# Bias products of the first half moved behind its conditioning passes, with the selection tree in SBUF and a reordered last step

## The reference, cut to what matters

```
w = weights[subjects]; b = bias[subjects]
h = einsum('bct,bcd->bdt', x, w) + b[:, :, None]
gate = silu((h @ q(gate_w)) * gate_scale)
up = (h @ q(up_w)) * up_scale
out = x + ((gate * up) @ q(down_w)) * down_scale     # q: round to float8_e4m3
```

## Time and profile before

| | us |
|---|---|
| time, median of 3 runs (lowest to highest) | 50.13 (50.04 to 50.27) |
| the profiled execution's own time | 50.52 |
| its span, first to last instruction | 48.6 |
| PE busy | 43.6 (90%) |
| DVE busy | 39.0 (80%) |
| ACT busy | 26.3 (54%) |
| POOL busy | 9.8 (20%) |

### The profile page before, as it was taken

How to read it: one execution, slowest core, us unless ns; L and a number is a source line. 1 busy time by engine, 2 the same in 40 slices (tenths; PEclk the granted TensorE clock), 3 DMA queues, 4 the chain that set the end, 5 groups by cost and what they waited for, 6 DMA issues and landing times.

```text
span 48.6 us, 678 instructions
## 1 busy us (share of the span) xinstructions
PE 43.6 (90%) x201; PEld 33.6 (69%) x201; DVE 39.0 (80%) x74; ACT 26.3 (54%) x45; POOL 9.8 (20%) x19
## 2 busy tenths in 40 slices
PE   1999899999999999999999999999999999998000
PEld 1331499997788878888788887888878888976000
DVE  2828899699899999899998999997659495985900
ACT  0945406984559684597319695631845728870000
POOL 3028904049910003930000000000000000370000
PEclk9999999999999999999999999999999999999997
DMA  0499999999950000000000000000000000028093
GB/s 0 101 316 391 357 390 379 416 410 414 410 223 7 0 0 0 0 0 0 0 0 13 7 0 0 0 0 0 0 0 0 0 0 7 0 89 332 10 333 99
DMA packets 2995, 5.71 MB, mean 118 GB/s; under 512 B 432, under 2 KB 1072, under 8 KB 2992
## 3 DMA queue, kind: packets, MB, share of 16 engines
q1 hardware_dynamic: 2704, 5.53, 30.9%
q10 hardware_dynamic: 288, 0.15, 1.1%
HBM read 4.63 MB, written 1.05 MB: 117 GB/s over the span
## 4 chain that ended last, share of the span: by engine, by line
PE 81%; DMA 5%; POOL 3%; DVE 2%; issue 1%; DVEq 1%; POOLq 0%
PE gu L552 46%; PE acc L560 23%; PE acc L525 8%; DMA const_in<-in_consts_dram 5%; PE acc L516 3%; DVE res L454 2%; POOL bias_tok L327 2%; DVEq L70 1%; POOL bias_r L320 1%; POOL bias_r L318 0%; POOLq L323 0%; POOLq L317 0%
## 5 line engine op out<-in xcount | busy, mean ns | idle before, releaser
L552 PE MATMUL gu<-h_hi,w_q 128*128 128x512 f32 (+1 forms) x52 | 15.2, 378 | 0.0
L552 PE MATMUL gu<-h_lo,w_q 128*128 128x512 f32 (+1 forms) x52 | 15.1, 377 | 0.0
L281 ACT CAST f_hi<-fuse 128x512 fp32r<-128x512 f32 (+1 forms) x13 | 7.6, 587 | 10.5 <-DVE fuse L441 10.5
L449 DVE TENSOR_TENSOR f_lo<-fuse,f_hi 128x512 fp32r<-128x512 f32 (+1 forms) x13 | 8.8, 675 | 3.2 <-ACT f_hi L281 3.2
L552 PEld LDWEIGHTS gu<-h_hi,w_q 128*128 128x128 f32 x52 | 9.5, 187 | 2.1
L552 PEld LDWEIGHTS gu<-h_lo,w_q 128*128 128x128 f32 x52 | 9.4, 187 | 2.2 <-DVE h_lo L421 0.2
L441 DVE SCALAR_TENSOR_TENSOR fuse<-gu,const_in,silu 128x512 f32<-128x512 f32 (+1 forms) x13 | 9.2, 706 | 0.4 <-ACT silu L274 0.4
L274 ACT ACTIVATE silu<-gu,const_in 128x512 f32<-128x512 f32 (+1 forms) x13 | 8.5, 651 | 1.1 <-PE gu L552 1.1
L560 PE MATMUL acc<-f_lo,w_q 128*128 128x512 f32 (+1 forms) x26 | 8.0, 381 | 0.0
L560 PE MATMUL acc<-f_hi,w_q 128*128 128x512 f32 (+1 forms) x26 | 7.8, 376 | 0.0
L239 ACT ACTIVATE w_big<-w_big,big_least 128x768 f32<-128x768 f32 (+2 forms) x8 | 6.2, 770 | 0.5 <-DVE w_big L358 0.5
(11 more groups left out here) (37 smaller groups left out, 24.7 us busy)
## 6 DMA issues: line engine op xcount, KB each, us to landing
w_in<-in_weights_dram SPq DMA_DIRECT2D x4, 384.0 KB, 6.2
x_tok<-in_x_by_time_dram SPq DMA_DIRECT2D x1, 1024.0 KB, 8.9
out_dram<-res SPq DMA_DIRECT2D x3, 256.0 KB, 2.1
x_sb<-in_x_dram SPq DMA_DIRECT2D x1, 512.0 KB, 3.6
w_in<-in_weights_dram SPq DMA_DIRECT2D x2, 256.0 KB, 4.0
x_sb<-in_x_dram SPq DMA_DIRECT2D x2, 256.0 KB, 4.2
w_in<-in_weights_dram SPq DMA_DIRECT2D x2, 128.0 KB, 4.9
const_in<-in_consts_dram SPq DMA_DIRECT2D x1, 151.0 KB, 2.4
```

Of the source, the lines that this page charges most:

```text
L281: nc.scalar.copy(f_hi[:, s % SLOTS, cols], fuse[:, s % SLOTS, cols]).then_inc(f_hi_made, 1)
L449: nc.vector.tensor_tensor(f_lo[:, s % SLOTS, cols], fuse[:, s % SLOTS, cols], f_hi[:, s % SLOTS, cols].bitcast(F32), ALU.subtract).then_in ...
L552: last = nc.tensor.matmul(gu[:, (s + q) % 2, part, cols], w_q[:, i, col:col + P], h[:, n, k, cols], start=(v == 0 and k == 0), stop=(v == ...
```

## The change

The first half's conditioning products now open the accumulator, its bias products stand behind them and close it, and `h_made` goes up after each of these bias products. Nine zero matmuls become eleven. Half 0's tree moves from PSUM to SBUF, its even part is shared between ACT (three of four pairs) and POOL (one), and one block of half 0's placement goes from ACT to POOL. The bias split moves from POOL to DVE, where one of the two mask operations goes away. POOL spreads the bias of half 0, places its block, and only then spreads that of half 1. In the last step both pieces of gate and up run without a break; `down` is reordered so that block b = 0 of the last half is complete before b = 1; `finish(0, 1)` stands behind DVE's last two subtractions, `y_sc` behind ACT's last two roundings, and the store of POOL's result is issued by ACT.

```diff
-    WARM = 9
+    WARM = 11
-        tree = [... for t in (gu_flat[:, 512:1024], tree_sb)]
+        tree = [tree_sb[:, n].rearrange("p (q g d) -> p q g d", g=GH, d=D) for n in range(HALVES)]
-        ACT_BLOCKS = ((0, 1), (0,))
-        POOL_BLOCKS = ((), (1, 2))
+        ACT_BLOCKS = ((0,), (0,))
+        POOL_BLOCKS = ((1,), (1, 2))
@@ sync
-            sp.wait_ge(res_pool, 1)
-            store(0, 0, TOK)
@@ scalar, front
-            for n in range(HALVES):
-                nc.scalar.copy(tree[n], cond_rep[:, :, 0]...).then_inc(tree_even[n], 1)
+            nc.scalar.copy(tree[0][:, 0:PAIRS - 1], cond_rep[:, 0:PAIRS - 1, 0]...).then_inc(tree_even[0], 1)
+            nc.scalar.copy(tree[1], cond_rep[:, :, 0]...).then_inc(tree_even[1], 1)
@@ scalar, last step
-            silu_of(s, 0, PIECES[0])
+            for q in range(LAST):
+                silu_of(s, q, PIECES[q])
+            for q in range(LAST):
+                round_of(s, q, PIECES[q])
             act.wait_ge(y0_made, 1)
             nc.scalar.activation(y_sc[:], acc[:, 0], ACT.Copy, scale=down_col[:, 0:1]).then_inc(y_scaled, 1)
-            silu_of(s, 1, PIECES[1])
-            for q in range(LAST):
-                round_of(s, q, PIECES[q])
+            act.wait_ge(res_pool, 1)
+            act.dma_start(out_rows[:, 0, 0:TOK], res[:, 0, 0]).then_inc(stored, 16)
@@ gpsimd
-            nc.gpsimd.tensor_copy(bias_r[:], bias_in).then_inc(bias_hi_made, 1)
-            nc.gpsimd.tensor_tensor(bias_r[LO_ROW:2 * LO_ROW], ..., ALU.subtract).then_inc(bias_lo_made, 1)
-            for n in range(HALVES):
-                place_bias(n)
+            nc.gpsimd.tensor_copy(tree[0][:, PAIRS - 1], cond_rep[:, PAIRS - 1, 0]...).then_inc(tree_even[0], 1)
+            place_bias(0)
+            place(0)
+            place_bias(1)
+            place(1)
@@ vector, front
+            nc.vector.tensor_copy(bias_r[:], bias_in).then_inc(bias_hi_made, 1)
+            nc.vector.tensor_tensor(bias_r[LO_ROW:2 * LO_ROW], ..., ALU.subtract).then_inc(bias_lo_made, 1)
-            for bits in (bits_ps, bits_sb):
-                nc.vector.tensor_tensor(bits[:], ..., ALU.bitwise_and).then_inc(bits_made, 1)
+            nc.vector.tensor_tensor(bits_ps, ..., ALU.bitwise_and).then_inc(bits_made, 1)
@@ vector, last step
-            fuse_of(s, 0, PIECES[0])
+            for q in range(LAST):
+                fuse_of(s, q, PIECES[q])
+            for q in range(LAST):
+                rest_of(s, q, PIECES[q])
             finish(0, 1)
-            fuse_of(s, 1, PIECES[1])
-            for q in range(LAST):
-                rest_of(s, q, PIECES[q])
@@ tensor, bias_of(n)
-                                     start=True, stop=False, skip_group_check=True)
+                    last = nc.tensor.matmul(..., start=(n == 1), stop=(n == 0), skip_group_check=True)
+                    if n == 0:
+                        last.then_inc(h_made, 1)
@@ tensor, condition(n)
-                                                start=False, stop=(g == GH - 1), skip_group_check=True)
-                    last.then_inc(h_made, 1)
+                                                start=(n == 0 and g == 0), stop=(n == 1 and g == GH - 1), ...)
+                    if n == 1:
+                        last.then_inc(h_made, 1)
-            for n in range(HALVES):
-                bias_of(n)
-                condition(n)
+            condition(0)
+            bias_of(0)
+            bias_of(1)
+            condition(1)
@@ tensor, last step
-            gate_up(s, 0, PIECES[0])
+            for q in range(LAST):
+                gate_up(s, q, PIECES[q])
             for b in range(TB):
                 down_block(s - 2, 0, b)
                 down_block(s - 2, 1, b).then_inc(y0_made, 1)
-            gate_up(s, 1, PIECES[1])
+            for v in range(2):
+                down_block(s - 1, v, 0)
             for q in range(LAST):
+                down_block(s, 0, 0, PIECES[q])
+                if q == LAST - 1:
+                    down_block(s - 1, 0, 1)
+                last = down_block(s, 1, 0, PIECES[q])
+            last.then_inc(y1_made, 1)
+            down_block(s - 1, 1, 1)
+            for v in range(2):
+                last = down_block(s, v, 1)
+            last.then_inc(y1_made, 1)
```

More of the change, by code:

```diff
@@ L97, in adaln_ffn @@
         cond_bd = sb("cond_bd", [P, G, P])
-        tree_sb = sb("tree_sb", [P, TOK])
-        bits_sb = sb("bits_sb", [P, BITS, G], I32)
+        tree_sb = sb("tree_sb", [P, HALVES, TOK])
         bias_r = sb("bias_r", [P, D], F32R)
@@ L116, in adaln_ffn @@
         warm_ps = gu[:, 0, 0]
-        gu_flat = gu.rearrange("p s w c -> p (s w c)")
-        tree = [t.rearrange("p (q g d) -> p q g d", g=GH, d=D) for t in (gu_flat[:, 512:1024], tree_sb)]
+        tree = [tree_sb[:, n].rearrange("p (q g d) -> p q g d", g=GH, d=D) for n in range(HALVES)]
         bits_ps = gu[:, 1, 1, 0:BITS * G].bitcast(I32).rearrange("p (k g) -> p k g", g=G)
@@ L244, in _ @@
             act.wait_ge(const_ld, 16)
-            for n in range(HALVES):
-                nc.scalar.copy(tree[n], cond_rep[:, :, 0].unsqueeze(2).to_broadcast([P, PAIRS, GH, D])
-                               ).then_inc(tree_even[n], 1)
+            nc.scalar.copy(tree[0][:, 0:PAIRS - 1], cond_rep[:, 0:PAIRS - 1, 0].unsqueeze(2).to_broadcast([P, PAIRS - 1, GH, D])
+                           ).then_inc(tree_even[0], 1)
+            nc.scalar.copy(tree[1], cond_rep[:, :, 0].unsqueeze(2).to_broadcast([P, PAIRS, GH, D])
+                           ).then_inc(tree_even[1], 1)
             def place(n):
@@ L317, in _ @@
             pool.wait_ge(const_ld, 16)
-            nc.gpsimd.tensor_copy(bias_r[:], bias_in).then_inc(bias_hi_made, 1)
[L319 to L323, removed]
+            nc.gpsimd.tensor_copy(tree[0][:, PAIRS - 1], cond_rep[:, PAIRS - 1, 0].unsqueeze(1).to_broadcast([P, GH, D])
+                                  ).then_inc(tree_even[0], 1)
             def place_bias(n):
@@ L329, in place_bias, with place @@
                                         ALU.mult).then_inc(bias_placed, 1)
-            for n in range(HALVES):
-                place_bias(n)
-            pool.wait_ge(bd_zeroed, 1)
[L336 to L340, removed]
+            def place(n):
+                pool.wait_ge(tree_level[n], BITS)
+                for j in POOL_BLOCKS[n]:
+                    nc.gpsimd.tensor_copy(*block_of(n, j)).then_inc(cond_placed[n], 1)
+                pool.wait_ge(cond_placed[n], J)
+            pool.wait_ge(bias_pick_made, 1)
+            pool.wait_ge(bias_lo_made, 1)
+            place_bias(0)
+            pool.wait_ge(bd_zeroed, 1)
+            pool.wait_ge(bias_placed, 1)
+            place(0)
+            place_bias(1)
+            pool.wait_ge(bias_placed, 2)
+            place(1)
             for e, (i, lo, hi) in enumerate(POOL_PIECES):
@@ L380, in _ @@
             nc.vector.tensor_copy(ones_r[:], ones_f[:]).then_inc(ones_made, 1)
-            dve.wait_ge(subj_in, 16)
-            dve.wait_ge(bit_set, BITS)
-            for bits in (bits_ps, bits_sb):
-                nc.vector.tensor_tensor(bits[:], subj_i[:, 0:G].unsqueeze(1).to_broadcast([P, BITS, G]),
-                                        bit_of[:].unsqueeze(2).to_broadcast([P, BITS, G]),
-                                        ALU.bitwise_and).then_inc(bits_made, 1)
+            dve.wait_ge(const_ld, 16)
+            nc.vector.tensor_copy(bias_r[:], bias_in).then_inc(bias_hi_made, 1)
+            dve.wait_ge(bias_hi_made, 1)
+            nc.vector.tensor_tensor(bias_r[LO_ROW:2 * LO_ROW], bias_in[LO_ROW:2 * LO_ROW],
+                                    bias_r[LO_ROW:2 * LO_ROW].bitcast(F32), ALU.subtract).then_inc(bias_lo_made, 1)
+            dve.wait_ge(subj_in, 16)
             dve.wait_ge(iota_made, 2)
@@ L391, in _ @@
                                     ALU.is_equal).then_inc(bias_pick_made, 1)
+            dve.wait_ge(bit_set, BITS)
+            nc.vector.tensor_tensor(bits_ps, subj_i[:, 0:G].unsqueeze(1).to_broadcast([P, BITS, G]),
+                                    bit_of[:].unsqueeze(2).to_broadcast([P, BITS, G]),
+                                    ALU.bitwise_and).then_inc(bits_made, 1)
             def select(n):
@@ L398, in select @@
                     if k == 0:
-                        dve.wait_ge(tree_even[n], 1)
+                        dve.wait_ge(tree_even[n], 2 - n)
                         to = tree[n]
@@ L406, in select @@
                         data = tree[n][:, step:PAIRS:2 * step]
-                    mask = (bits_sb if n == 0 and k > 0 else bits_ps)[:, k, groups].unsqueeze(1).unsqueeze(3).to_broadcast([P, left, GH, D])
+                    mask = bits_ps[:, k, groups].unsqueeze(1).unsqueeze(3).to_broadcast([P, left, GH, D])
                     nc.vector.copy_predicated(to, mask, data).then_inc(tree_level[n], 1)
-            dve.wait_ge(const_ld, 16)
-            dve.wait_ge(bits_made, 2)
+            dve.wait_ge(bits_made, 1)
             select(0)
```

(34 more changed lines are left out.)

## The result

| | before | after |
|---|---|---|
| time, median (lowest to highest) | 50.20 us (50.04 to 50.34) | 51.27 us (51.15 to 52.07) |
| ratio to before, 95% interval | | 1.0216 (1.0167 to 1.0265) |
| span of the profiled execution | 48.6 | 49.3 |
| its own time | 50.52 | 51.37 |

The change makes the kernel 1.07 us slower; 51.1 was forecast.

A forecast was written before the change was run, and what follows sets the result against it. The chain TensorE, ACT, DVE, TensorE ahead of the first gate product was taken to decide: front +1.05, tail -0.05, so 51.1 us on the median of 50.13. Range 50.5 to 51.45 us.

The forecast's parts named there:

- Start of conditioning: Half 0's conditioning on TensorE, set by half 0's placement: starts at about 6.1 us, 0.05 earlier (ends: 0.15 earlier, 0.3 later).
- The bias products: Moved behind half 0's conditioning, they delay ACT's copy of h and so the first gate product: +1.05 us (0.85 to 1.3).
- The sum: Profiled execution's own time 50.52 + 1.0 = 51.5; it lies 0.39 above the median of 50.13, so 51.1 on the median.
- The cover: TensorE's two further bias products (0.47 us) lie under ACT's delay; without that cover they would cost about 0.4.
- The tail: Last step: DVE's chain ends 0.67 us earlier, but final stores give back almost all: -0.05 (ends -0.67 and +0.1).
- The rate formula: End of span: when the last stores' data is ready, plus 1.8 us fixed, plus bytes over 377 GB/s; 48.55 forecast.
- A: Rival at the final stores: they don't bind, so the tail gives its 0.67 us; 50.5 us, chance 0.10.
- B: Rival: tail outweighs front, if `high_of_h(0, 0)` starts before 8.4 and the front costs under 0.67; 49.85 us, chance 0.04.
- C: Rival: TensorE's full clock comes later because it idles between the zeros and conditioning; 52.2 us, chance 0.05.
- D: Rival in half 0's placement: DVE and POOL lock each other out, or a late tree; +0.15, 51.25 us, chance 0.07.

## Why the prediction was right

**What decides.** The line that the forecast was built on, TensorE's eighth product, ACT's copy, `big(0)`, DVE's two passes, gate product, is the one that the trace of after shows. The move alone (+1.9%) and the changed kernel without it (+0.05%) frame it from both sides, and reordering ACT's list takes most of it off.

**Start of conditioning.** "About 6.1, 0.05 earlier": 6.05. The 0.05 can't be told from scatter: with the old front conditioning starts at 6.14, 6.11 and 6.04 in three traces, with the new one at 6.05 to 6.10. The masked copies start at 3.87 (3.85 forecast), the blocks are over by 5.99 (6.0). The Trainium skill's rule of a lock between DVE's and GpSimd's copies ("SBUF — State Buffer", Who interferes with whom) didn't show: POOL's copy ran from 5.58 to 5.89 beside DVE's two in 0.47 us. No run shows whether DVE's copies were in the two-port mode that the rule is about.

**The bias products.** +1.05 was forecast for the gate product. At equal pace the runs show +1.01 (11.27 against 10.26) or +0.96 (against 10.31, the old front with the stores spread). Against the trace of before it is only +0.63, and my absolute times of the front were 0.4 to 0.5 us late (ACT 8.84 forecast, 8.37 measured; idle ahead of `add_big(0)` 1.6 forecast, 1.12 measured), because of the one thing that I had left where it was: the moment at which TensorE reaches its upper clock. Of the zero matmuls still running at 4.7 us, the trace of after has

```profile
L515 PE MATMUL gu<-warm x3: 379/390/601, 4.4 to 5.0; 128*128 128x512 bf16 x3
```

(ns, shortest, median and longest), so the pace changes there at about 4.8 us, not 7. Conditioning ran wholly at 2.4 GHz, 1.8 us for sixteen products in place of the 2.21 of the earlier trace rows. It is no effect of the change, as the last section shows. The trace of before was the odd one: its span is 48.6 us, and 40 of the 46 executions of that kernel that were measured beside the experiments have 48.1 to 48.3. The sum had taken off 0.39 for that execution without knowing its cause. So the forecast of the median compares kernels on one footing, and the +1.05 holds there; the comparison of the two traces alone would not have shown it.

The cover named for TensorE's two further bias products was real. They "would cost by themselves about 0.4"; with ACT's order put right they cost about 0.3.

**The tail.** "DVE's chain ends 0.67 earlier": 0.70 between old and new tail in the changed kernel, and all four `finish` operations run on end, so DVE did wait for neither block, as forecast. Between the traces of before and after it is 0.63, and the 0.07 of difference is not the tail's: with the old tail in the changed kernel DVE ends 35.60 behind the first gate product, 35.53 in the kernel before. "The transfers give back almost all, -0.05": in the changed kernel the span behind the gate product is 38.01 with the old tail and 38.03 with the new one, so they give back all of it, as far as spans given to 0.1 us can tell. The rate formula held: `finish(0, 1)` ended at 43.86 + 0.75 = 44.61, and 44.61 + 1.8 + 2.78 (1.05 MB at 377 GB/s) is 49.2 against a span of 49.3; with one store less it gives 44.63 + 1.8 + 2.09 (0.79 MB) = 48.5 against 48.6. Its rate of 377 is the best half microsecond, though; from 45.5 to 48.0 it was 324 to 377. The Trainium skill's rule quoted beside it, that DMAs of both issuing engines share 16 engines and interleave ("Trainium Kernel Development and Optimization", Key Constraints), agrees with the trace: with stores of both queues under way the engines moved 373 GB/s at most, and 377 in the half microsecond from 45.5, at whose start ACT's first store was only being issued.

**Rivals.** A (the tail gives 0.67): refuted by the old tail and by the store left out. B (the front costs under 0.67): its sign, ACT's copy before 8.4, came true (8.37), and yet the front cost 1.0. The sign was an absolute time, badly chosen: with the bias ahead the copy starts at 7.25 at this pace. With ACT's order kept it starts 0.04 us behind the product that releases it in each of these traces. C (a late clock by the gap): no run shows it. Its nearest test is nine zeros, whose executions kept in the ratio lie between 51.08 and 51.20 us; but in the profiled one the pace had changed ahead of the gap, so what a gap does before that moment stays open. D (lock): not seen. The chances have a slip: forecast, A, C and D add up to 0.92 for slower, which leaves 0.04 for no change, not 0.91 and 0.05.

## What to carry to other kernels

A product that is moved from idle time behind the work cost its own engine only 0.3 us here; the rest of the 1.0 us came from the semaphore that moved with it. Ask of each counter that now rises later which instruction waits for it, and what stands behind that instruction in its engine's list. The shorter chain ahead of the final stores was worth nothing, because it gathered the stores into one burst: so sum the bytes that leave after the first late result, divide by the rate, and compare.

## What the runs showed of the hardware

The moment at which TensorE's products go over to the faster pace moved by 3 us between executions that had done the same on TensorE up to the earliest of these moments: zero matmuls on end from 0.99 us. It was at about 7 us in the trace of before, 6.7 in the one with the bias behind each block, 4.8 in that of after, and ahead of 4.0 in those with the old tail and with nine zeros, here the latter:

```profile
L515 PE MATMUL gu<-warm x4: 379/418/634, 3.1 to 4.0; 128*128 128x512 bf16 x4
```

The number of zeros doesn't order them: with nine it was at 7 and ahead of 4.0, with eleven at 6.7, 4.8 and ahead of 4.0. What sets the moment stays open. A single pair of traces can so show a front 0.4 us shorter or longer than it is. The granted clock in the windows reads 1.00 from the start in all of them and doesn't show it; the pace of equal products does.
